# Four chained convolution layers on one core: constant matmuls in two stretches of TensorE's queue, and the sum of relus in another order

## The reference

```
x = x + L0(gn(x))     # 16 bases: a 1x1 and a 3x3 conv give weights per pixel for 16 3x3 convs
x = x + L1(gn(x))     # nine taps at fractional offsets (bilinear): four slots after mixing
x = x + L2(gn(x))     # four experts, below
x = x + L3(gn(x))     # conv3x3, bn, relu, conv3x3, bn, relu(. + x); kernels mixed of ten
```

```
y = relu(bn(conv3x3(masked, w1[e]) + b1[e]))
y = bn(conv3x3(y, w2[e]) + b2[e])        # call this z
out = out + relu(z + gn(x))
```

## Time and profile before

| | us |
|---|---|
| median of 3 runs | 425.21 (425.14 to 425.44) |
| the profiled execution | 425.92 |
| its span | 424.1 |
| PE busy in the span | 382.5 (90%) |
| DVE / ACT / POOL busy | 276.4 / 57.3 / 91.1 |
| mean granted clock of PE | 0.966 |
| chain that ended last, by engine | PE 75%, DVE 11%, SPq 5%, DMA 4%, issue 3%, ACT 2%, POOL 1% |

### The profile page before, as it was taken

The page is one execution under the profiler, slowest core; times in us unless marked ns, Lnnn a source line. Parts: engine busy times, 40 slices in busy tenths (PEclk is TensorE's granted clock), DMA queues, the critical chain, the costliest instruction groups (busy, mean ns, idle before and its releaser), DMA issues.

```text
span 424.1 us, 8245 instructions
## 1 busy us (share of the span) xinstructions
PE 382.5 (90%) x3174; PEld 259.1 (61%) x3174; DVE 276.4 (65%) x486; ACT 57.3 (14%) x95; POOL 91.1 (21%) x220
## 2 busy tenths in 40 slices
PE   0799799999999999999999999479999979889892
PEld 0344588888888888888888888312247652157570
DVE  4981377777877888887787798844444077831155
ACT  0721000000000000000000000041013027552200
POOL 6687500688800000000000000105000037000000
PEclk9999799999999999999999999859999999899997
DMA  6276758055455545535613400068900000000023
GB/s 204 61 182 153 186 142 220 7 144 130 120 123 125 146 104 139 151 86 143 162 49 96 109 2 0 1 152 195 218 19 2 3 2 0 2 2 5 3 79 123
DMA packets 19649, 40.17 MB, mean 95 GB/s; under 512 B 7328, under 2 KB 8224, under 8 KB 19040
## 3 DMA queue, kind: packets, MB, share of 16 engines
q1 hardware_dynamic: 18848, 38.63, 35.9%
q10 hardware_dynamic: 768, 1.08, 1.0%
HBM read 4.62 MB, written 2.10 MB: 16 GB/s over the span
## 4 chain that ended last, share of the span: by engine, by line
PE 75%; DVE 11%; SPq 5%; DMA 4%; issue 3%; ACT 2%; POOL 1%; DVEq 0%; POOLq 0%; ACTq 0%
PE ps L734 21%; PE ps L735 21%; PE ps L736 7%; PE ps L777 7%; PE ps L914 4%; PE ps L900 4%; PE ps L850 2%; DMA LS<-HS 2%; DMA X<-in_x 2%; PE ps L871 2%; SPq L379 2%; SPq L364 2%; PE ps L790 2%; DVE RED L974 1%; PE ps L840 1%
## 5 line engine op out<-in xcount | busy, mean ns | idle before, releaser
L734 PE MATMUL ps<-WA,HS 128*128 128x512 f32 x396 | 160.3, 405 | 1.7 <-DMA LS<-HS 1.7
L735 PE MATMUL ps<-WB,LS 128*128 128x512 f32 x396 | 157.6, 398 | 0.0
L992 DVE TENSOR_TENSOR PROD<-ps,PT 128x512 f32<-128x512 f32 x132 | 91.1, 690 | 46.2 <-PE ps L736 41.8
L974 DVE TENSOR_REDUCE RED<-PROD 128x32 f32<-128x512 f32 x132 | 89.1, 675 | 0.0
L734 PEld LDWEIGHTS ps<-WA,HS 128*128 128x128 f32 x396 | 75.5, 191 | 21.0 <-issue 1.8
L735 PEld LDWEIGHTS ps<-WB,LS 128*128 128x128 f32 x396 | 75.6, 191 | 16.5
L736 PE MATMUL ps<-WC,TS 96*128 96x512 f32 x132 | 52.7, 399 | 0.0
L628 ACT ACTIVATE P<-ps 128x256 f32 x15 | 5.8, 385 | 207.5 <-PE ps L749 207.5
L449 POOL MEMSET IMG<- 128x67 f32 x1 | 0.2, 154 | 155.5 <-DVE X L981 155.5
L777 PE MATMUL ps<-SK,WE 128*32 128x512 f32 x256 | 29.2, 616 | 0.0
L736 PEld LDWEIGHTS ps<-WC,TS 96*128 96x128 f32 x132 | 25.1, 190 | 5.9
(11 more groups left out here) (189 smaller groups left out, 336.2 us busy)
## 6 DMA issues: line engine op xcount, KB each, us to landing
HS<-HI SPq DMA_DIRECT2D x72, 96.5 KB, 2.1
LS<-HS SPq DMA_DIRECT2D x6, 1158.0 KB, 6.8
TS<-LO SPq DMA_DIRECT2D x72, 80.0 KB, 2.1
SK<-IMG SPq DMA_DIRECT2D x32, 131.8 KB, 2.6
HS<-LO SPq DMA_DIRECT2D x24, 96.5 KB, 2.1
LS<-LO SPq DMA_DIRECT2D x24, 96.5 KB, 2.2
X<-in_x SPq DMA_DIRECT2D x4, 512.0 KB, 5.8
out_x<-OT SPq DMA_DIRECT2D x8, 256.0 KB, 2.0
```

What stands on the lines that cost most here:

```text
L734: pe.matmul(ps[b][:, :], px(HS, dy * PW), WA[:, dy, :], start=(dy == 0), stop=False)
L735: pe.matmul(ps[b][:, :], px(LS, dy * PW), WB[:, dy, :], start=False, stop=False)
L974: ve.tensor_reduce(RED[j % 2][:, 32 * b:32 * b + 32], PROD[b % 2][:, :].rearrange("p (o e) -> p o e", e=E0), AX.X, ALU.add).then_inc(sum_d ...
L992: ve.tensor_tensor(PROD[b % 2][:, :].rearrange("p (o e) -> p o e", e=E0), ps[b][:, :].rearrange("p (o e) -> p o e", e=E0), para.rearrange( ...
```

## The change

- Behind block 0: `fill` is defined earlier and takes a bank. PE waits for bank 7's last reader and for the constants, runs `fill(4)`, then the last `back`, then `fill(10)`.
- The fill in front of the second masked convolution becomes 13 instead of 12, the one behind it 9 instead of 8, the one before the relus 3 instead of 8.
- POOL: five more instructions make EMASK (a one where a partition belongs to expert e); the product for W3 moves ahead of both powers of the batch norms.
- ZE: 16 copies of one pixel read the raw convolution in PSUM (`raw_z`), spread over the waits of the second batch norm; scale and bias are applied to ZE afterwards, with the pair of each partition picked by EMASK. Row 6 (Z6) goes.
- The full z banks: VectorE writes those of experts 2 and 3, ACT those of 0 and 1, both behind their first relus. PE no longer waits for all four; the groups take copy banks by a table.
- The loop: group (6, 8) goes last; the relu of the edge rows moves to ACT (one in each of groups 2 to 5), their sum and its addition to X to POOL; statistics are taken at other places, the last three at the end.
- The end: PE's `fill(7)` waits for all eight groups, and a `fill(4)` behind `coef_ready` follows; between L3's two convolutions there is a `fill(3, 0)` into bank 0.

```diff
-RELU_ROWS = ((8, 16), (16, 24), (24, 32), (32, 40), (6, 8), (40, 48), (48, 56), (56, H - 1))
+RELU_ROWS = ((8, 16), (16, 24), (24, 32), (32, 40), (40, 48), (48, 56), (56, H - 1), (6, 8))
-IDLE_BANKS = (4, 5, 6, 7, 0, 1)
+Z_ORDER = (2, 3, 0, 1)
+COPY_BANKS = (4, 5, 6, 7, 4, 5, 6, 7) + (0, 1, 4, 5, 6, 7) * 4
...
 POOL
+            step(gp.memset(EMASK[:, :], 0.0))
+            for e in range(NE):
+                step(gp.memset(EMASK[32 * e:32 * e + 32, e:e + 1], 1.0))
...
-            gp.wait_ge(bn_input_ready, 1)
-            gp.tensor_tensor(Q2[:, 7, 1:2], ..., ALU.pow).then_inc(bn_power_done, 1)
-            gp.wait_ge(bn_input_ready, 4)
-            gp.tensor_tensor(Q2[:, 4, :], ..., ALU.pow).then_inc(bn_power_done, 1)
             gp.wait_ge(w3_in_sbuf, 4)
             gp.tensor_tensor(W3[:, 0, :, :], W3[:, 0, :, :], SROW..., ALU.mult).then_inc(w3_mixed, 1)
+            (the four lines removed above)
             gp.wait_ge(norm2_done, 1)
-            gp.wait_ge(z_row6_done, NE)
+            def edge_rows(n):
+                e = Z_ORDER[n]
+                if n < 2:
+                    gp.wait_ge(z_by_vector, n + 1)
+                else:
+                    gp.wait_ge(z_by_scalar, n - 1)
+                gp.tensor_tensor(T2[e][:, 0:6 * W], U[:, 0:6 * W], Z[:, e, 0:6 * W], ALU.add)
+                gp.tensor_tensor(T2[e][:, 6 * W:7 * W], U[:, (H - 1) * W:PIX], Z[:, e, 7 * W:8 * W], ALU.add).then_inc(edge_rows_step, 1)
+            edge_rows(0)
+            edge_rows(1)
+            gp.wait_ge(z_by_scalar, 2)
             (edge columns, with row 6 of Z for Z6)
-            for e in range(NE):
-                gp.wait_ge(z_done, e + 1)
-                (the same two additions).then_inc(first_rows_added, 1)
+            for n in range(2, NE):
+                edge_rows(n)
+            gp.wait_ge(edge_rows_relu, 2)
+            T2[2] += T2[3]          (448 pixels each)
+            gp.wait_ge(edge_rows_relu, 4)
+            T2[0] += T2[1]
+            T2[0] += T2[2]
+            X[:, 0:6 * W] += T2[0][:, 0:6 * W]; X[:, (H - 1) * W:PIX] += T2[0][:, 6 * W:7 * W], each .then_inc(edge_rows_added, 1)
...
 ACT
-            for e in range(NE):
-                act.wait_ge(z_row6_done, e + 1)
-                act.activation(Z[:, e, :], ps[e][:, :], ACT.Identity, bias=..., scale=...).then_inc(z_done, 1)
             act.wait_ge(z_by_expert, 1)
             for i in range(N_RELU):
                 (relus of images 1 to 3)
+                if i == 0:
+                    z_full(0)
+                    z_full(1)
+                elif 2 <= i < 2 + NE:
+                    act.wait_ge(edge_rows_step, i - 1)
+                    act.activation(T2[Z_ORDER[i - 2]][:, 0:7 * W], T2[Z_ORDER[i - 2]][:, 0:7 * W], ACT.Relu).then_inc(edge_rows_relu, 1)
...
 PE
+            pe.wait_ge(block0_in_sbuf, STEPS * STRIP_T)
+            pe.wait_ge(mix_ready, 1)
+            fill(4)
             back(REST - 1, NT - 1, STEPS)
+            fill(10)
...
-            fill(12)
+            fill(13)
...
-            fill(8)
+            fill(9)
...
-            fill(8)
+            fill(3)
             copy_experts(0)
-            pe.wait_ge(z_row6_done, NE)
-            pe.wait_ge(z_done, NE)
             for i in range(N_RELU):
                 if i + 1 < N_RELU:
                     copy_experts(i + 1)
                 pe.wait_ge(relu_by_vector, i + 1)
                 pe.wait_ge(relu_by_scalar, (B - 1) * (i + 1))
-                if i >= 2:
+                if i < 2:
+                    pe.wait_ge(z_by_vector, i + 1)
+                else:
                     pe.wait_ge(x3_rows_done, i - 1)
...
-            pe.wait_ge(x3_rows_done, N_RELU - 1)
+            pe.wait_ge(x3_rows_done, N_RELU)
             fill(7)
-            pe.wait_ge(x3_rows_done, N_RELU)
+            pe.wait_ge(coef_ready, 3)
+            fill(4)
...
+            pe.wait_ge(hidden3_by_scalar, 1)
+            fill(3, 0)
             pe.wait_ge(hidden3_by_vector, 4)
...
 DVE
+            def raw_z(e):
+                for b in range(B):
+                    ve.tensor_copy(ZRAW[32 * e:32 * e + 32, b:b + 1], ps[e][32 * b:32 * b + 32, 6 * W + 1:6 * W + 2])
...
             ve.tensor_copy(Q2[:, 0, :], M2[:, :, 0]).then_inc(bn_input_ready, 1)
+            raw_z(0)
             ve.wait_ge(averaged, 1)
...
+            raw_z(1)
             ve.wait_ge(averaged, 2)
...
+            raw_z(2)
+            raw_z(3)
             ve.wait_ge(bn_power_done, 2)
...
-            (four row-6 instructions and 16 copies to ZE)
+            step(ve.tensor_tensor(QE[:, :, :], Q2[:, 5:7, :], EMASK..., ALU.mult))
+            step(ve.tensor_reduce(QD[:, :], QE[:, :, :], AX.X, ALU.add))
+            ve.tensor_scalar(ZE[:, :], ZRAW[:, :], QD[:, 0:1], QD[:, 1:2], ALU.mult, ALU.add).then_inc(z_by_expert, 1)
...
             relu_share(0)
+            for e in Z_ORDER[0:2]:
+                ve.tensor_scalar(Z[:, e, :], ps[e][:, :], Q2[:, 5, e:e + 1], Q2[:, 6, e:e + 1], ALU.mult, ALU.add).then_inc(z_by_vector, 1)
             for i in range(N_RELU):
                 if i + 1 < N_RELU:
                     relu_share(i + 1)
+                if i == 4:
+                    ve.wait_ge(edge_cols_added, 1)
+                for k in {4: (1,), 5: (2, 3), 6: (4,), 7: (5,)}.get(i, ()):
+                    ve.wait_ge(x3_rows_done, k)
+                    stats3(k)
                 (add the sum to X).then_inc(x3_rows_done, 1)
-                (rows_of_edge for two experts at i = 3 and two at i = 5; statistics at i = 2, 3, 4, 6, 7)
+            ve.wait_ge(x3_rows_done, N_RELU - 1)
+            stats3(N_RELU - 2)
+            ve.wait_ge(edge_rows_added, 2)
+            stats3(N_RELU - 1)
+            ve.wait_ge(x3_rows_done, N_RELU)
+            ins = stats3(0)
```

More of the change, by code:

```diff
@@ L138, in build @@
         SDIAG = sb("SDIAG", [P, C])[0]
+        EMASK = sb("EMASK", [P, NE])[0]
         ID = sb("ID", [P, P])[0]
@@ L764, in block0, with fill @@
                         back(TIT - 1, g - 1)
+            def fill(n, bank=7):
+                for _ in range(n):
+                    pe.matmul(ps[bank][:, 0:2 * P], ONE[:, :], REPL[:, :, :].rearrange("p (a b) c -> p a (b c)", a=1).broadcast_to([P, 2, P]), start=True, stop=True)
             pe.wait_ge(w0_split, 4)
@@ L827, in _ @@
             pe.matmul(ps[4][:, 6 * C:7 * C], ONE[:, :], SDIAG[:, :], start=True, stop=True).then_inc(w3_summed, 1)
-            def fill(n):
-                for _ in range(n):
-                    pe.matmul(ps[7][:, 0:2 * P], ONE[:, :], REPL[:, :, :].rearrange("p (a b) c -> p a (b c)", a=1).broadcast_to([P, 2, P]), start=True, stop=True)
             fill(7)
@@ L864, in copy_experts @@
                 for b in range(B):
-                    use = 4 * i + b - len(IDLE_BANKS)
-                    if use >= 0 and use % B == 0:
+                    uses = [n for n in range(4 * i + b) if COPY_BANKS[n] == COPY_BANKS[4 * i + b]]
+                    use = uses[-1] if uses else -1
+                    if use < 0 and i > 0:
+                        pe.wait_ge(z_by_scalar, 2)
+                    elif i > 0 and use % B == 0:
                         pe.wait_ge(relu_by_vector, use // B + 1)
-                    elif use >= 0:
+                    elif i > 0:
                         pe.wait_ge(relu_by_scalar, use // B * (B - 1) + use % B)
```

65 lines of the change are left out of this document (26 added, 39 removed).

## The result

| | before | changed |
|---|---|---|
| median of all runs of the comparison (20 each) | 425.17 | 422.94 |
| lowest, highest | 420.65, 428.66 | 416.48, 428.03 |
| profiled execution | 425.92 | 420.92 |
| its span | 424.1 | 419.1 |
| mean granted clock | 0.966 | 0.983 |

The ratio of the compared runs is 0.9889, with a 95% interval of 0.9848 to 0.9930: 1.1% faster, 425.17 x 0.0111 = 4.7 us. The ratio compares the runs near the quickest of each kernel, and the times of both kernels spread over 8 to 12 us, so that by the medians of all runs it is 2.2 us. What that spread is turned out to be half of the lesson.

A forecast was written before the change was run, and what follows sets the result against it. PE was taken to run at half clock behind block 0, with row copies limiting the gain. Gains 1.9 - 0.2 + 3.1 + 1.2 = 6.0 from the median 425.21 gave 419.2 us; range 417.5 to 422.0.

The forecast's parts named there:

- Part 1: Matmuls behind block 0: fills keep the clock up, gaining 3.4 us, of which row copies let 1.9 be kept.
- the charge of 0.5 us for ACT's copies beside SP's: Ahead of the sixth convolution: ACT's copies, moved forward, delay SP's last nine by 0.5 us, between ends 0 and 1.9.
- Rival B: Behind block 0: ACT's copies hold up SP's, nothing kept in front, 421.1 us; chance 0.12.
- rival C: Behind block 0: fills do not hold the clock over the pieces, 0.5 later instead of 1.9 earlier, 421.6 us; chance 0.11.
- Part 2: Batch norms: bn2_ready 0.2 us later, experts' vector 3.1 us gained by the step, 2.9 net; both fills hidden.
- Part 3: Loop, from experts' vector to last statistics: 21.35 us instead of 22.6, 1.2 us gained.
- Rival A: New loop: the clock falls at its start or end, costing 1.3 us, so 420.5, both 421.8; chance 0.25.
- my own sign of being wrong: Wrong if the clock line has a new dip in the 33rd to 36th slice, or PE waits for z_by_vector.
- the walk: Loop: step-by-step timing from measured durations, with ACT pacing at 2.35 us an iteration and last statistics ending at 369.05.
- Part 4: The end: fill(7), fill(4) and fill(3, 0) cost 0, without cover; ends +0.3 and +0.2 us.
- Rival D: Loop: the clock falls as it begins and stays down, eight iterations cost 10 us, 429 us; chance 0.04.

The follow-up runs named there:

- the bridge: Changed kernel plus two constant matmuls between the second batch norm's two averaging matmuls and one behind the second; median 423.17 us, ratio 0.9911.
- merged copies: Changed kernel with SP's 32 row copies made into 16 of twice the rows, same bytes: median 429.82 us; with the bridge also, 426.54.
- ACT's copies later and earlier: Changed kernel with ACT's 16 row copies behind the second layer's fourth (later) or second (earlier) convolution instead of the third; medians 422.75 and 423.89 us.
- the loop alone: Changed kernel with all fills as in the kernel before, keeping the raw copies and the loop's new order and shares; median 422.34 us, ratio 0.9949.

## Why the prediction was right, and where it was not

**By the numbers**, 419.2 was forecast; the compared runs give 425.17 x 0.9889 = 420.5, the profiled execution 420.9, in the range. The median of all runs, 422.9, is above its end. The sum was right for an execution like the profiled one, and said too little of what the others do.

**Part 1, the mechanism right in the profiled execution, the kept part mis-sized.** The clock stayed up, and the pieces came out at 1.14, 0.62, 1.15 where 1.10, 0.60, 1.10 stood. The fifth addition comes 28.6 us behind the last reduce instead of 31.7: 3.1 of the 3.4 us. The step that failed is the charge of 0.5 us for ACT's copies beside SP's, with the landing of 2.8 behind it. The 2.8 was the median of all copies; the last one, for which PE waits, had landed 3.57 us behind its issue already in the trace of before, at 301.8 and not at 301.0. Beside ACT's it landed after 4.96 us in one trace and 5.67 in the other, so that 0.9 us were kept in the first and 1.1 lost in the second. I had taken the row of landings at 3.1 over the rule of the Trainium skill (DMA: Bandwidth & Descriptors, Issuing engines are not separate DMA queues), by which transfers from different queues interleave on the same engines. These traces agree with the rule: issued beside ACT's the last copy landed after 4.96 and 5.67 us, with ACT's moved back after 3.4. My estimate by it, 9 us in place of 6 for SP's last copies, was too high: the last landing took 1.4 and 2.1 us longer than in the trace of before, and in the first of these traces both queues together moved 264 GB/s over 6 us, more than the 200 of one.

Rival B (nothing kept) had 0.12 and was nearer to the runs as a whole: of the complete changed loop, with the bridge or without, 44 runs with the front fills have a mean of 422.8 and 24 without them one of 421.3; of the kernel before, 12 runs with them 427.7 and 35 without 424.9. The ratios do not show such a loss for the changed loop. Three things in the traces go against the fills in front. The clock did not always hold behind them (rival C, in four of eight traces). Without them it was at half for 10.2 us in three traces, not 13.7, so that 2.3 to 2.6 us and not 3.1 are to be had up to the fifth addition. And in each of the six traces of the changed loop with front fills and unmerged copies the clock fell once more between 342 and 354, and in three of them again at the fills ahead of L3; in the two without front fills and with three fills ahead of the relus it did not, and vector to L3 took 23.5 us in place of 24.6 to 28.6; nor did it in the two kernels with merged copies, which have the front fills, and in which the clock was at half for 10.2 us around their long wait. Why a long half-clock stretch early on goes with a full clock in the loop is open, and with one trace of each kernel it may be chance.

**Part 2, right.** Forecast 2.9, measured 2.8, and from the eighth addition to the vector every trace with the changed batch norms takes 34.0 to 34.1 us. The product at 0.16, the raw copies of 0.16 each (eight in 1.34), both fills of 13 and 9 hidden.

**Part 3, the sum right by luck: two errors cancel.** Forecast 21.35 from vector to last statistics, measured 21.50. Rival A (0.25) happened, but one stretch before where I looked: the clock fell at 344, behind the averages with their gaps, and 1.5 us were lost before the first relu. By my own sign of being wrong, a new dip in the 33rd to 36th slice, this part was wrong. That the gaps let the clock fall is likely and not shown, since other traces with the same gaps kept it. In return the walk was 1.3 us too slow: ACT's iteration is 2.18 and not 2.35, and the traces without a dip in the loop need 20.1. The edge relu itself is 0.58 to 0.66, near the 0.56 taken. POOL ends at 365.93 (forecast 365.9).

**Part 4.** fill(4) and fill(7) cost 0.1 in the profiled execution. In three other traces (the bridge, ACT's copies later and earlier) they ran partly at the half clock and were on the path, 4.9 us from the last statistics to L3 in place of 3.4: the price that rival A had named, 1.3, measured as 1.5. I took fill(3, 0) as worth nothing because the clock was up there in the trace of before; in the trace of the loop alone its absence goes with 20.57 - 18.89 = 1.7 us, and the absence of fill(4) at the end of the loop with as much in the second trace of the kernel before with the front fills. One trace each, and other traces without these fills kept the clock: that the fills would have prevented it is not shown.

**Rival D** did not come. Rival C did not come in the profiled execution and came in part in others, as above. That the change was faster holds for every comparison of the complete kernel, though by less than 2% and in the second one by 0.1 to 1.2%; which of its parts is, does not follow the forecast: the loop and the changed batch norms carry it (422.34 alone against 425.29), not the clock behind block 0, on which I had spent most of the working.

## What to carry to other kernels

Before filling PE's idle time to keep its clock, ask what the quicker stretch will wait for next, and take the landing of the very transfer that is waited for, not the median of its like. A chain filled by a queue's issues does not tell whether the issues or the bytes are the limit; two kernels do, one with half of the copies and one with half of the bytes in some of them, and here both limits were close to each other. A stretch that one trace shows at full clock is no evidence that its gap is harmless, nor that its fill works; take two or three traces of the same kernel, and compare the whole spread of the times. Rearranging work so that an engine waits for less (16 copies into gaps, a vector scaled afterwards) gave its forecast gain in every trace.

## What was not expected of the hardware

- The same program runs in 416.5 to 428.0 us on one core, and the places of the half-clock stretches differ from trace to trace: in block 0, behind block 0, at 344, in the loop, ahead of L3, in either of the last two convolutions. Block 0 alone makes 3.4 us of it: four traces have no half-clock stretch near 50 us and their last reduce ends at 268.3 to 268.8, six have one of 3.4 us and end at 270.1 to 271.0, four have one of 6.8 us (before and changed among them) and end at 271.2 to 271.7. Nothing in the change touches that part.
- Fills that run without a gap ahead of a stretch do not secure its clock: 2.77 us of matmuls in 5.20 us stood behind the fills of the changed kernel's second trace, and then it fell. In the first trace the same stretch had 2.97 in 5.40 and it stayed.
- Copies from SBUF to SBUF of one queue went at 200 GB/s over 16 us with 263.8 KB each and at 177 (before, the same 16 us) to 202 with 131.8 KB; while two queues were active, 264 GB/s passed in 6 us, yet the copy that was waited for landed after 4.96 instead of 3.57 us:

```profile
276.00:292.00 16.00, 13.57 (x217) 3.83 (x220) 7.62 (x13) 5.14 (x10) 4.46 (x3) 1.00 0.81 182
294.00:300.00 6.00, 5.92 (x56) 1.71 (x48) 1.94 (x4) 0.00 (x0) 0.26 (x1) 1.00 1.00 264
```

- The kernel with half of the bytes in SP's second part had the narrowest spread, 419.4 to 421.2, though from six runs only.
